# Attention scores from two fp32r parts in two 64-row tiles of the array, in a decoder layer on one core

## The chip, the cores and the metric

The kernel runs on one core of one Trainium2 chip. The metric is the device time of one execution in microseconds (us). A core has TensorE (PE in the profile; its weight loads are PEld), VectorE (DVE), ScalarE (ACT), GpSimd (POOL) and SyncE (SP), which here only issues transfers.

## The reference

A decoder layer with a layer norm behind each of three parts: causal self-attention, cross-attention to 64 context rows, and a mixture of 16 experts (4 picked per token) with one shared expert. The change touches the self-attention alone.

```python
# x: (2, 1024, 256); 16 heads of 16 columns
Q = einsum('bsd,hkd->bhsk', x, WQ)   # K, V alike
scores = einsum('bhqd,bhkd->bhqk', Q, K) / sqrt(16)
scores = where(causal, scores, -inf)
attn = einsum('bhqk,bhkv->bhqv', softmax(scores), V)
x = layernorm(x + einsum('bhsv,hdv->bsd', attn, WO))
x = layernorm(x + cross_attention(x, ctx, mask))
x = layernorm(x + experts(x))
```

## The kernel before

**Heads and groups.** The 2x16 heads are worked in `NG` = 8 groups of `HG` = 4. Q and K are projected in float32 (L1029), and their results are cut into three bfloat16 parts each: ACT copies PSUM to part 0 (L566), DVE subtracts it (L732, `rest`), ACT copies the rest to part 1 (L571), POOL subtracts again to part 2 (L443). SP stores each result to HBM (`qk_parts`, L373) and loads from there the stacks of a group (`load_stack`, L369): 16 rows per part, six pairs of parts under each other, `KR` = 96 rows. A matmul over the 96 rows gives Q times K from parts (`SPLIT_Q`, `SPLIT_K`), for one head.

**Two passes over the scores.** The softmax needs row maxima. The *A jobs* (PE L973) compute scores with queries on the partitions, add the causal mask on diagonal blocks with a matmul of the identity and a mask (L978), and DVE takes the negative maxima (L701). The maxima are cut in parts, transposed (*M*: L711 to L721 on DVE, L1001 on PE, L594 on ACT) and written by SP as three more rows under the Q stack (`KM` = 99). The *B jobs* (L991) compute the scores again with keys on the partitions, for a pair of heads into two banks; with the three extra rows they come out less their maximum; on diagonal blocks L994 adds the mask; ACT takes the exponential (L585). The *V products* (L1015) multiply with V in float32, four heads in four 32-column tiles of the array, each of them as two instructions in the profile.

**Order.** `step_order` writes out one group for all engines: 24 slots with one B job each, and in them the A jobs of the *next* group: a head of `A_HEAD` = 4, the other 34 spread over 18 slots. An A job is (query tile i, key half c, width w, first head, heads in a bank); there are 38 a group. They use three PSUM banks, `A_BANKS`, in turn; PE waits before job n for the maxima of jobs up to n-3 (L970). A V product follows every second slot from slot 3 on, M stands after slot 19. PE, ACT and DVE each run the same list in order. B job n waits for the exponential n-2. The A jobs of group 0 stand in the projection stage (`P1`), six in each half step of a Q or K projection.

**Loops.** `groups` runs group 0, then a hardware loop (`Fori`) with two passes of three groups, then group 7. `blocks` does the same for the experts: block 0 written out, a loop over blocks 1 to 3. SP loads the stacks two groups ahead.

Of the kernel before, what the change touches and what calls it, by code (L numbers as in the profile page):

```python
# [21 lines left out]
F32 = mybir.dt.float32  # L22
# [28 lines left out]
SPLIT_Q = (0, 1, 2, 0, 1, 0)  # L51
SPLIT_K = (0, 0, 0, 1, 1, 2)
KR = len(SPLIT_Q) * DH
KM = KR + 3
# [83 lines left out]
def build(nc, a, out, qk_parts, l_dram):  # L138
    with ExitStack() as ctx:
# [21 lines left out]
        qs = stacks[:, 8192:14336].bitcast(BF16).rearrange("p (u h s) -> p u h s", u=3, h=HG)  # L161
        ks = stacks[:, 14336:20480].bitcast(BF16).rearrange("p (u h s) -> p u h s", u=3, h=HG)
# [6 lines left out]
        parts = temps[:, 0:3072].bitcast(BF16).rearrange("p (u s t) -> p u s t", u=2, s=3)  # L169
        rest = temps[:, 3072:5120].rearrange("p (u t) -> p u t", u=2)  # L170
# [44 lines left out]
        nmx = sb("neg_max", [P, NC, HG, TB], F32)  # L215
        nm = sb("neg_m", [P, 2, HG * TB], F32)
        mparts = sb("m_parts", [P, 3, HG * TB], BF16)
        mrow = sb("m_rows", [3 * HG * TB, P], BF16)
# [21 lines left out]
        hs = nc.alloc_sbuf_tensor_at("h_split", [P, SPLIT_BUFS, 2, CH], F32R, offset=temps_at + 4 * 3072)  # L240
        ps = ctx.enter_context(nc.psum_tensor("ps", [P, 8, CH], F32))
# [11 lines left out]
        qk_ready, part_a, resid, part_b, part_c = (sem(n) for n in ("qk_ready", "part_a", "resid", "part_b", "part_c"))  # L253
# [45 lines left out]
        def groups(eng, run):  # L299

            run(0, 0, STEP0, 0)
            with eng.Fori(0, (NG - 2) // 3) as r:
                for s in range(3):
                    run(r * 3 + (s + 1), (s + 1) % 3, STEP, r + (s + 2) // 3)
            run(NG - 1, (NG - 1) % 3, LAST, 0)

        def blocks(eng, run):


            run(0, 2)  # L310
            with eng.Fori(1, T // CH) as c:
                run(c, 0)
# [34 lines left out]
        def _(sp):  # L347
# [13 lines left out]
            for dst, name in ((identb, "identb"), (causA, "causA"), (causB, "causB")):  # L361
                sp.dma_start(dst[:], a[name]).then_inc(ld_caus, 16)

            def load_stack(g):
                b, o, g2 = g // GB, g % GB // 2, g % 2
                for t, dst, split in ((0, qs, SPLIT_Q), (1, ks, SPLIT_K)):
                    for at, part in enumerate(split):
                        src = qk_parts[t, b, o, part, 64 * g2:64 * g2 + 64, :].rearrange("(h r) n -> r h n", h=HG)
                        sp.dma_start(dst[at * DH:(at + 1) * DH, g % 3], src).then_inc(ld_stack[g % 3], 16)  # L369

            for n, (b, o, t) in enumerate(QK):
                sp.wait_ge(part_c, n + 1)
                sp.dma_start(qk_parts[t, b, o].rearrange("s p n -> p s n"),  # L373
                             parts[:, n % 2]).then_inc(stored[n % 2], 16)
# [7 lines left out]
            for g in range(NG):  # L382
                sp.wait_ge(m_row, g + 1)
                for s in range(3):
                    n = HG * TB
                    sp.dma_start(qs[KR + s:KR + s + 1, g % 3].rearrange("o h s -> o (h s)"),
                                 mrow[s * n:(s + 1) * n, :]).then_inc(m_loaded, 16)
                if g == 0:
# [5 lines left out]
                    for dst, name in ((x, "x"), (wo1, "wo1"), (wxq, "wxq"), (wxk, "wxk"), (wxv, "wxv"),  # L394
                                      (wxo, "wxo"), (ctxT, "ctxT"), (bq, "bq"), (bk, "bk"), (bv, "bv"), (bo, "bo"),
                                      (gw, "gw"), (gb, "gb"), (mask_words, "mask"), (identf, "identf"), (hm, "hm")):
# [31 lines left out]
        def _(pool):  # L428

            nc.gpsimd.memset(ks[KR:P], 1.0).then_inc(filled, 1)  # L430
# [10 lines left out]
            for n in range(NQK):  # L441
                pool.wait_ge(part_b, n + 1)
                nc.gpsimd.tensor_tensor(parts[:, n % 2, 2, :], rest[:, n % 2, :], parts[:, n % 2, 1, :],  # L443
                                        ALU.subtract).then_inc(part_c, 1)
                g = n - 4
                if 0 <= g < 3:
                    pool.wait_ge(v_kept, NVJ // B)
# [847 lines left out]
```

## Time and profile before

| | us |
|---|---|
| median of 3 runs | 797.43 (796.6 to 802.91) |
| span of the profiled execution | 794.0 |
| projection stage, until the first B job | 0 to 79.5 |
| eight groups | 79.5 to 331 |
| the rest (output projection, cross-attention, experts) | 331 to 794 |

The span is that of one profiled execution, from its first to its last instruction. A time on a timeline row counts from the span's start. A matmul's record lasts longer than its columns take, since the pipeline is in it; how fast matmuls follow each other is read from their starts. Idle time in brackets is that of the engine ahead of the instruction, with what released it.

### The profile page before, as it was taken

What the parts mean: (1) busy time and instruction counts of PE and PEld (TensorE: products, weight loads), DVE (VectorE), ACT (ScalarE), POOL (GpSimd) and SP (SyncE); (2) the same over time, 40 slices, a digit from 0 to 9 for tenths busy, and PEclk for the clock granted to TensorE, in tenths of its full rate; (3) what the DMA queues carried; (4) which work ended last, traced back from release to release, by engine and by line L of the source; (5) the groups of instructions that cost most, each with busy time, mean ns of one, the idle gap of its engine ahead of it and who ended that gap; (6) DMA issues with size and microseconds to landing.
All of it is one profiled execution on the core that took longest, in us unless ns stands there. A gap on an engine that the chain in (4) does not pass through costs nothing.

```text
span 794.0 us, 13785 instructions
## 1 busy us (share of the span) xinstructions
PE 738.2 (93%) x4632; PEld 493.8 (62%) x4632; DVE 555.3 (70%) x1195; ACT 381.0 (48%) x639; POOL 280.6 (35%) x285
## 2 busy tenths in 40 slices
PE   6688999999699999988999998999999999999994
PEld 3345443443344443444777787877888888888883
DVE  1287867868386683195788774699778768777777
ACT  2222666566365667623544444654444544545441
POOL 8323001141204204223013223574445445545542
PEclk9989999999899999999999998999999999999998
DMA  4866951532506000080000000000000000000000
GB/s 150 161 164 158 254 104 27 84 63 37 96 4 96 17 3 18 17 320 32 1 2 1 1 1 1 1 2 1 1 1 14 13 0 0 26 0 0 7 20 27
DMA packets 21311, 38.23 MB, mean 48 GB/s; under 512 B 5768, under 2 KB 9320, under 8 KB 20872
## 3 DMA queue, kind: packets, MB, share of 16 engines
q1 hardware_dynamic: 19688, 35.32, 19.4%
q0 software_dynamic: 1568, 2.18, 1.2%
q8 instruction: 34, 0.56, 0.3%
q14 instruction: 21, 0.17, 0.1%
HBM read 28.64 MB, written 8.65 MB: 47 GB/s over the span
## 4 chain that ended last, share of the span: by engine, by line
PE 74%; DVE 13%; issue 5%; DMA 3%; ACT 3%; SPq 1%; POOL 1%; POOLq 0%; DVEq 0%; ACTq 0%
PE ps L1119 18%; PE ps L1217 9%; PE ps L1015 9%; PE ps L991 9%; PE ps L973 8%; PE ps L1137 4%; PE ps L1156 3%; DVE neg_max L701 3%; DVE x_tok L876 3%; PE ps L1146 2%; PE ps L1171 2%; PE ps L994 2%; PE ps L978 2%; PE ps L1029 2%; DMA stacks<-qk_parts 1%
## 5 line engine op out<-in xcount | busy, mean ns | idle before, releaser
L701 DVE TENSOR_REDUCE neg_max<-ps 128x1 f32<-128x512 f32 (+3 forms) x304 | 180.7, 655 | 72.0 <-PE ps L978 58.8
L1119 PE MATMUL ps<-x_split,w_split 128*128 (+1 forms) x816 | 201.6, 396 | 1.7 <-DVE temps L858 1.2
L585 ACT ACTIVATE temps<-ps 128x1024 f32<-128x1024 f32 (+1 forms) x192 | 149.0, 811 | 100.8 <-PE ps L994 74.3
L1119 PEld LDWEIGHTS ps<-x_split,w_split 128*128 128x128 f32 x816 | 149.9, 189 | 32.5 <-issue 2.5
L511 POOL TENSOR_TENSOR w_split<-stacks,w_split 128x512 fp32r<-128x512 f32 x70 | 90.8, 1297 | 130.3 <-ACT w_split L618 130.3
L973 PE MATMUL ps<-stacks 96*128 96x512 bf16 (+3 forms) x384 | 106.0, 334 | 21.6 <-issue 8.4
L1217 PE MATMUL ps<-w_split,h_split 128*128 128x256 f32 x816 | 110.5, 285 | 6.1 <-DVE x_tok L876 5.2
L1217 PEld LDWEIGHTS ps<-w_split,h_split 128*128 128x128 f32 x816 | 106.3, 190 | 15.0 <-issue 8.1
L876 DVE SCALAR_TENSOR_TENSOR x_tok<-ps,o_norm,x_tok 128x256 f32<-128x256 f32 x256 | 105.6, 475 | 0.1
L991 PE MATMUL ps<-stacks 99*128 99x512 bf16 (+3 forms) x384 | 99.9, 330 | 1.8 <-ACT temps L585 1.1
L624 ACT ACTIVATE temps<-ps 128x512 f32<-128x512 f32 x68 | 40.8, 599 | 112.9 <-PE ps L1119 112.7
L858 DVE TENSOR_TENSOR temps<-ps,temps 128x512 f32<-128x512 f32 x68 | 47.0, 691 | 60.9 <-ACT temps L624 60.6
L1015 PE MATMUL ps<-temps,v_group 128*32 128x512 f32 (+3 forms) x768 | 81.8, 498 | 0.0
L991 PEld LDWEIGHTS ps<-stacks 99*128 99x128 bf16 x384 | 33.8, 98 | 76.8 <-ACT temps L585 49.9
L973 PEld LDWEIGHTS ps<-stacks 96*128 96x128 bf16 x384 | 37.3, 100 | 61.9 <-DVE neg_max L701 25.5
L864 DVE TENSOR_TENSOR h_split<-temps,h_split 128x512 fp32r<-128x512 f32 x68 | 61.7, 908 | 6.3 <-ACT h_split L629 6.3
L505 POOL TENSOR_TENSOR ln_rstd<-ln_var_eps,minus_half 128x1 f32<-128x1 f32 x32 | 19.1, 598 | 122.8 <-DVE ln_var_eps L774 122.8
L518 POOL TENSOR_TENSOR w_split<-stacks,w_split 128x256 fp32r<-128x256 f32 x68 | 55.0, 809 | 13.8 <-ACT w_split L630 13.8
L629 ACT ACTIVATE h_split<-temps 128x512 fp32r<-128x512 f32 x68 | 43.1, 634 | 34.9 <-DVE temps L858 33.9
L978 PE MATMUL ps<-caus_a,ident_b 128*128 128x128 bf16 x256 | 51.1, 226 | 0.0
L994 PE MATMUL ps<-caus_b,ident_b 128*128 128x128 bf16 x256 | 50.2, 220 | 0.0
L643 ACT ACTIVATE temps<-temps 128x512 f32<-128x512 f32 x32 | 20.2, 631 | 50.8 <-DVE temps L890 50.8
(120 smaller groups left out, 887.3 us busy)
## 6 DMA issues: line engine op xcount, KB each, us to landing
stacks<-qk_parts SPq DMA_DIRECT2D x96, 128.0 KB, 5.7
qk_parts<-temps SPq DMA_DIRECT2D x8, 768.0 KB, 4.1
stacks<-in_w SPq DMA_DIRECT2D x1, 4352.0 KB, 14.0
stacks<-in_w SPq DMA_DIRECT2D x1, 2176.0 KB, 19.0
x_T<-in_xT SPq DMA_DIRECT2D x4, 512.0 KB, 8.9
x_tok<-in_x SPq DMA_DIRECT2D x1, 2048.0 KB, 12.4
out_tokens<-x_tok SPq DMA_DIRECT2D x16, 128.0 KB, 1.7
temps<-row_sums POOLq DMA_DIRECT2D x28, 64.0 KB, 2.6
```

The costliest lines, as they stand in the source:

```text
L511: nc.gpsimd.tensor_tensor(w13s[:, split_buf(n), 1].rearrange("p k n -> p (k n)"), w13[:, n % NE], w13s[:, split_buf(n), 0].rearrange("p k ...
L585: nc.scalar.activation(pt[:, n % 4, :, 0:w], ps[:, 2 + 2 * (n % 2):4 + 2 * (n % 2), 0:w], ACT.Exp, scale=SCALE).then_inc(b_exp, 1)
L701: nc.vector.tensor_reduce(nmx[:, c, h0:h0 + nh, i], ps[:, A_BANKS[n % 3], 0:w * nh].rearrange("p (h k) -> p h k", h=nh), axis=AX.X, op=ALU ...
L864: nc.vector.tensor_tensor(hs[:, split_buf(e), 1], hT[:, e % 2, :], hs[:, split_buf(e), 0], ALU.subtract).then_inc(h_lo, 1)
L876: nc.vector.scalar_tensor_tensor(x[:, t, :], y, comb[:, 1, t, e:e + 1], x[:, t, :], ALU.mult, ALU.add).then_inc(y_added, 1)
L973: last = nc.tensor.matmul(ps[:, A_BANKS[n % 3], w * s:w * s + w], qs[0:KR, ua, h0 + s, P * i:P * i + P], ks[0:KR, ua, h0 + s, CH * c:CH * ...
L978: last = nc.tensor.matmul(ps[:, A_BANKS[n % 3], w * (s + 1) - P:w * (s + 1)], identb[:], causA[:], start=False, stop=True)
L991: last = nc.tensor.matmul(ps[:, bank, 0:w], ks[0:KM, u, 2 * pr + s, P * j:P * j + P], qs[0:KM, u, 2 * pr + s, q0:q0 + w], start=True, stop ...
L994: last = nc.tensor.matmul(ps[:, bank, 0:P], identb[:], causB[:], start=False, stop=True)
L1015: last = nc.tensor.matmul(ps[HS * h:HS * h + HS, 6, CH - w:CH], vg[:, u, j, h, :], pt[:, (2 * p + h // 2) % 4, h % 2, 0:w], start=(j == 0) ...
L1119: last = nc.tensor.matmul(ps[:, 2 * part + e % 2, :], w13s[:, split_buf(e), wp, k, P * part:P * part + P], xs[:, bass.ds(c, 1), xp, k, :], ...
L1217: last = nc.tensor.matmul(ps[:, Y_BANKS[e % 2] + i // 2, D * (i % 2):D * (i % 2) + D], hs[:, split_buf(e), hp, P * i:P * i + P], w2s[:, sp ...
```

## The change

- Q and K are cut into two parts in fp32r (float32 storage, 4 bytes): ACT copies, DVE subtracts, and that is all. Three pairs of parts make `KR` = 48 rows, with two rows for the maxima `KM` = 50. A stack holds two heads side by side on the partitions: rows 0 to 63 and 64 to 127. The memory of a stack and the size of its load (twelve transfers of 128 KB) are the same; SP writes four rows of maxima, not three. A store of a projection grows from 768 KB to 1 MB.
- A score matmul reads 48 (50) rows of one half. The two heads of a pair follow each other as matmuls on rows 0 and 64, into two banks. Their mask matmuls (128 rows) come behind both; those of A take all blocks of a bank at once.
- An A job is now for a pair of heads and fills two banks, so there are 20 a group with 40 maxima; the head is 2 jobs, the rest one a slot, 3 in each half step of `P1`. PE waits before job n for maxima up to unit 2n-2.
- The chain of the maxima has three steps on DVE, not five; the transpose is float32.
- `Fori` is gone: seven groups and four expert blocks are written out. POOL's part of the cut is gone, its copies of V stand ahead in one piece, its first memset covers all of the K stack in float32.

```diff
-SPLIT_Q = (0, 1, 2, 0, 1, 0)
-SPLIT_K = (0, 0, 0, 1, 1, 2)
+SPLIT_Q = (0, 0, 1)
+SPLIT_K = (0, 1, 0)
 KR = len(SPLIT_Q) * DH
-KM = KR + 3
+KM = KR + 2
+ROWS = P // 2
+NPR = HG // 2
...
-            _n = min(HG, CH // _w)
-            A_JOBS += [(_i, _c, _w, _h, _n) for _h in range(0, HG, _n)]
+            _n = min(NPR, CH // _w)
+            A_JOBS += [(_i, _c, _w, _pr, _n) for _pr in range(0, NPR, _n)]
 NA = len(A_JOBS)
+NU = 2 * NA
-A_HEAD = 4
+A_HEAD = 2
...
-            with eng.Fori(0, (NG - 2) // 3) as r:
-                for s in range(3):
-                    run(r * 3 + (s + 1), (s + 1) % 3, STEP, r + (s + 2) // 3)
+            for g in range(1, NG - 1):
+                run(g, g % 3, STEP, (g + 1) // 3)
...
-            with eng.Fori(1, T // CH) as c:
+            for c in range(1, T // CH):
...
+                        src = qk_parts[t, b, o, part, 64 * g2:64 * g2 + 64, :].rearrange(
+                            "(pr d r) n -> d r pr n", pr=NPR, d=2)
+                        for d in range(2):
+                            rows = slice(ROWS * d + at * DH, ROWS * d + (at + 1) * DH)
+                            sp.dma_start(dst[rows, g % 3].bitcast(F32), src[d]).then_inc(ld_stack[g % 3], 16)
...
-            nc.gpsimd.memset(ks[KR:P], 1.0).then_inc(filled, 1)
+            nc.gpsimd.memset(ks[:].bitcast(F32), 1.0).then_inc(filled, 1)
...
-                nc.gpsimd.tensor_tensor(parts[:, n % 2, 2, :], rest[:, n % 2, :], parts[:, n % 2, 1, :],
-                                        ALU.subtract).then_inc(part_c, 1)
...
-                nc.scalar.activation(parts[:, n % 2, 1, :], rest[:, n % 2, :], ACT.Copy).then_inc(part_b, 1)
...
+                        for d in range(2):
+                            src = ps[:, A_BANKS[(2 * n + d) % 3], 0:w * npr].rearrange("p (h k) -> p h k", h=npr)
+                            nc.vector.tensor_reduce(nmx[:, c, d, pr:pr + npr, i], src,
+                                                    axis=AX.X, op=ALU.max, negate=True).then_inc(a_max, 1)
...
-                    dve.wait_ge(part_a, n + 1)
-                    if n >= 2:
-                        dve.wait_ge(part_c, n - 1)
+                    dve.wait_ge(part_hi, n + 1)
...
-                        wait(pe, a_max, (g + 1) * NA + (n - 1 if n < 2 else n - 2))
+                        wait(pe, a_max, (g + 1) * NU + max(2 * n - 1, 0))
                         diag = P * (i + 1) <= CH * (c + 1)
...
+                        banks = [A_BANKS[(2 * n + d) % 3] for d in range(2)]
+                        for s in range(npr):
+                            for d in range(2):
+                                rows = slice(ROWS * d, ROWS * d + KR)
+                                last = nc.tensor.matmul(ps[:, banks[d], w * s:w * s + w],
+                                                        qs[rows, ua, pr + s, P * i:P * i + P],
+                                                        ks[rows, ua, pr + s, CH * c:CH * c + w],
+                                                        start=(s == 0), stop=(s == npr - 1 and not diag))
+                        if diag:
+                            for d in range(2):
+                                edge = ps[:, banks[d], 0:w * npr].rearrange("p (h k) -> p h k", h=npr)[:, :, w - P:w]
+                                last = nc.tensor.matmul(edge, identb[:],
+                                                        causA[:].unsqueeze(1).to_broadcast([P, npr, P]),
                                                         start=False, stop=True)
...
+                        for d in range(2):
+                            rows = slice(ROWS * d, ROWS * d + KM)
+                            last = nc.tensor.matmul(ps[:, 2 + 2 * (n % 2) + d, 0:w], ks[rows, u, pr, P * j:P * j + P],
+                                                    qs[rows, u, pr, q0:q0 + w], start=True, stop=not diag)
+                        if diag:
+                            for d in range(2):
+                                last = nc.tensor.matmul(ps[:, 2 + 2 * (n % 2) + d, 0:P], identb[:], causB[:],
+                                                        start=False, stop=True)
```

## Rows read from the trace of the kernel before

**Rows 1.** The page's first part: busy us, share of the span, instructions.
```profile
PE 738.2 (93%) x4632; PEld 493.8 (62%) x4632; DVE 555.3 (70%) x1195; ACT 381.0 (48%) x639; POOL 280.6 (35%) x285
```

**Rows 2.** Windows: stretch, its length, busy us of each engine, clock, DMA.
```profile
112.00:140.00 28.00, 27.87 (x227) 11.80 (x229) 21.35 (x40) 18.62 (x26) 6.58 (x9) 1.00 0.37 58
300.00:330.00 30.00, 28.23 (x238) 10.31 (x236) 3.80 (x11) 23.80 (x34) 13.44 (x17) 1.00 0.08 22
```

**Rows 3.** L1001 on PE in three windows: durations, then first and last start.
```profile
L1001 PE MATMUL ps<-ident_b,m_parts x1: 257/257/257, 199.9 to 199.9; 128*96 128x128 bf16 x1
...
L1001 PE MATMUL ps<-ident_b,m_parts x1: 257/257/257, 240.3 to 240.3; 128*96 128x128 bf16 x1
...
L1001 PE MATMUL ps<-ident_b,m_parts x1: 257/257/257, 303.6 to 303.6; 128*96 128x128 bf16 x1
```

**Rows 4.** Timeline around the loop's jump: start, length, engine, what, idle before.
```profile
203.28 7.67 SPq L369 DMA_DIRECT2D stacks<-qk_parts  x12
207.31 0.23 PE L973 MATMUL ps<-stacks 96*128 96x128 bf16 x1 [3.50 <-issue]
...
211.76 0.27 PE L973 MATMUL ps<-stacks 96*128 96x128 bf16 x1 [4.05 <-issue]
```

**Rows 5.** Timeline of PE over one pair of slots.
```profile
128.52 1.06 PE L1015 MATMUL ps<-temps,v_group 128*32 128x512 f32 x8
129.52 0.60 PE L991 MATMUL ps<-stacks 99*128 99x512 bf16 x2
129.96 0.60 PE L973 MATMUL ps<-stacks 96*128 96x512 bf16 x2
...
131.35 0.22 PE L978 MATMUL ps<-caus_a,ident_b 128*128 128x128 bf16 x1
131.50 1.07 PE L1015 MATMUL ps<-temps,v_group 128*32 128x512 f32 x8
```

**Rows 6.** Timeline of PE in the head of a group.
```profile
140.48 0.23 PE L973 MATMUL ps<-stacks 96*128 96x128 bf16 x1
140.55 0.22 PE L978 MATMUL ps<-caus_a,ident_b 128*128 128x128 bf16 x1
...
142.00 0.34 PE L973 MATMUL ps<-stacks 96*128 96x384 bf16 x1 [0.20 <-DVE neg_max L701]
...
144.57 0.43 PE L1015 MATMUL ps<-temps,v_group 128*32 128x128 f32 x8
144.93 0.34 PE L991 MATMUL ps<-stacks 99*128 99x384 bf16 x1
```

**Rows 7.** Chain that ended last, in order of time: start, us, what.
```profile
471.10 1.69 PE ps L1189 x16
...
612.68 2.78 PE ps L1119 x12
615.47 1.43 PE ps L1217 x12
```

**Rows 8.** Timeline of DVE: the row maxima.
```profile
50.98 3.68 DVE L701 TENSOR_REDUCE neg_max<-ps 128x1 f32<-128x512 f32 x6 [0.63 <-PE ps L973]
...
130.38 1.29 DVE L701 TENSOR_REDUCE neg_max<-ps 128x1 f32<-128x512 f32 x2 [0.77 <-PE ps L973]
...
141.25 4.34 DVE L701 TENSOR_REDUCE neg_max<-ps 128x4 f32<-128x512 f32 x8 [4.71 <-PE ps L978]
```

**Rows 9.** Groups by form: busy us, mean ns, idle before and its releasers.
```profile
L701 DVE TENSOR_REDUCE neg_max<-ps 128x1 f32<-128x512 f32 x192 | 121.2, 682 | 17.5 <-PE ps L973 11.2 <-PE ps L978 6.0
...
L701 DVE TENSOR_REDUCE neg_max<-ps 128x1 f32<-128x384 f32 x64 | 32.0, 550 | 4.9 <-PE ps L978 4.8
```

**Rows 10.** Chain that ended last, in the projection stage.
```profile
20.25 1.07 ACT temps L571
21.38 2.14 POOL temps L443
23.54 3.55 DMA qk_parts<-temps
```

More of the change, by code:

```diff
@@ L360, in _ @@
             load_x(3)
[L361 removed]
+            for dst, name in ((identb, "identb"), (causA, "causA"), (causB, "causB"), (identf, "identf")):
                 sp.dma_start(dst[:], a[name]).then_inc(ld_caus, 16)
@@ L383, in _ @@
                 sp.wait_ge(m_row, g + 1)
[L384 to L387, printed above, removed]
+                for s in range(2):
+                    for d in range(2):
+                        n = NPR * TB
+                        at = ROWS * d + KR + s
+                        sp.dma_start(qs[at:at + 1, g % 3].rearrange("o pr s -> o (pr s)").bitcast(F32),
+                                     mrow[(2 * s + d) * n:(2 * s + d + 1) * n, :].bitcast(F32)).then_inc(m_loaded, 16)
                 if g == 0:
@@ L560, in _ @@
         def _(act):
-            def part_a_of(n):
+            for n in range(NQK):
                 act.wait_ge(qk_ready, n + 1)
@@ L592, in group @@
                         act.wait_ge(m_T, g + 2)
-                        wait(act, m_loaded, g * 48 + 48)
-                        nc.scalar.activation(mrow[:], ps[0:3 * HG * TB, 0, 0:64].bitcast(BF16),
-                                             ACT.Copy).then_inc(m_row, 1)
+                        wait(act, m_loaded, g * 64 + 64)
+                        nc.scalar.activation(mrow[:], ps[0:2 * HG * TB, 0, 0:P], ACT.Copy).then_inc(m_row, 1)
             groups(act, group)
@@ L985, in group @@
                         if n == 0:
-                            pe.wait_ge(m_loaded, g * 48 + 48)
+                            pe.wait_ge(m_loaded, g * 64 + 64)
                         wait(pe, b_exp, g * NB + n - 1)
                         diag = P * j >= CH * c
-                        for s in range(2):
-                            bank = 2 + 2 * (n % 2) + s
-                            last = nc.tensor.matmul(ps[:, bank, 0:w], ks[0:KM, u, 2 * pr + s, P * j:P * j + P],
-                                                    qs[0:KM, u, 2 * pr + s, q0:q0 + w], start=True, stop=not diag)
-                            if diag:
-                                last = nc.tensor.matmul(ps[:, bank, 0:P], identb[:], causB[:], start=False, stop=True)
+                        for d in range(2):
[3 more added lines that the diff above has]
+                        if diag:
+                            for d in range(2):
+                                last = nc.tensor.matmul(ps[:, 2 + 2 * (n % 2) + d, 0:P], identb[:], causB[:],
+                                                        start=False, stop=True)
                         last.then_inc(b_ready, 1)
```

104 lines of the change are left out of this document (39 added, 65 removed).

## Prediction

> **What bounds the kernel now.** I read the page's busy times first, then the windows, the times of one marker instruction, and last the timeline of TensorE (PE) and VectorE (DVE) in one attention group. Over the span PE is busy 93%, DVE 70%, ScalarE 48% [rows 1]. In the attention stage PE is busy 27.87 of 28.00 us, DVE 21.35 and ACT 18.62 [rows 2]. Only the last group differs: it has no A jobs, and there ACT has 23.80 us of 30 [rows 2].
>
> The transpose of the row maxima (L1001) runs eight times, once per group, and gives the period: 199.9 to 240.3 is 40.4 us, 240.3 to 303.6 is two groups of 31.65 us [rows 3]. The long one holds the jump back of the rolled loop: PE gets its next instructions 3.5 us late and stalls 4.05 us more inside the first A job, with nothing released by another engine, while twelve stack loads run [rows 4].
>
> The 31.65 us are PE's. In one pair of slots PE runs V (1.00 us), B, A, B, A without a hole: 131.50 minus 128.52 is 2.98 us [rows 5]. It is this pair that the change works on.
>
> **Prices from rows.** All in us.
> - A 512-column bf16 matmul streams in 0.217 (two in 0.43 to 0.44) [rows 5]; 128 columns with a mask matmul between take 0.06 each [rows 6].
> - fp32r runs at the same rate: 12 of 512 columns in 2.78. But 12 of 256 columns take 1.43, 0.119 each, and 16 of 16 columns with 128-column f32 weights 1.69, 0.106 each [rows 7]: below 256 columns a four-byte weight load sets the pace at 0.106.
> - V takes 0.36 at 128 columns and 1.00 at 512 [rows 5, 6]; the slope is (1.00-0.36)/384 = 1.67 ns a column, so 0.36 minus 0.213 = 0.15 is fixed. Before it, the last 128-column matmul started at 131.35 and was through at 131.41, V starts at 131.50: 0.09 more. V is the only place where the array changes its tiling (128x128 to 128x32 and back), so in costs 0.09 and out 0.15.
> - DVE: six 512-column maxima in 3.68 [rows 8], the first 0.68 long [rows 9], so 0.60 apart; 384 columns 0.55 long [rows 9]. 256 columns isn't in the trace; by those two I take 0.45.
> - Handing over: A matmuls at 129.96 and 0.22 later, DVE's first maximum at 130.38 [rows 5, 8]: 0.20 after the first one's last column. Back: DVE starts the first maximum at 141.25, ends it 0.68 later, and PE starts the A job that waited at 142.00 [rows 6, 8]: some 0.06.
>
> **The change part by part.**
> *Two heads at once.* Scores have 384+384 matmuls before and after; now neighbours lie in row tiles 0 and 64. I price a pair at 0.22 for any width: two weight loads of 0.106 one after the other, or 512 columns once. Bounds: 0.106 for narrow pairs if both tiles load at once, 0.43 if the tiles don't run together. The Trainium skill (TensorE: Matmul & The Clock Gate, Part 3) says that matmuls of different row groups start about 4 ns apart; no matmul of before uses a row tile, so no row here shows it, and the sum would be the same.
>
> *Switching.* Mask matmuls use all 128 rows. A diagonal job is now 64-row, 128-row, 64-row; 12 of 20 A jobs and 16 of 24 B jobs are diagonal. I take 0.09 in and 0.15 out, as at V [rows 5, 6], the nearest row; bounds are nothing, and 0.106 more at each pair where the weight load is exposed. The skill's page TensorEngine Tiling (Key Properties) says that changing the tiling mode drains the engine, which V's two gaps agree with; by it the switches cost, by a free change between row modes they don't, and that is a rival below.
>
> *Coarser A jobs.* This I take to be decisive. Before, 38 jobs use one bank each of three, and job n waits for the maximum n-3. Now a job fills two of the three banks, 20 jobs a group, and job n waits for unit 2n-2, the first half of the job just before it. PE can't be more than one job ahead. From one A job's last column to the next one's first column: 0.20+0.68+0.06 = 0.94. Then a pair: 1.16, raised to DVE's 2x0.60 = 1.20. A B job between hides in it (0.22, or 0.72 with its mask and three switches). In every second slot V stands between: 1.09+0.22+0.22 = 1.53. Two slots without masks: 2.73 to 2.98 before. The halved scores give 0.25 there, as PE's rest turns into waiting for DVE.
>
> With masks the steps grow. A job: 0.42 (pair 0.22, in 0.09, mask 0.11); a two-pair job 0.74; a B job after V 0.57 (0.42 and out 0.15). V with both gaps: 1.09, 0.88, 0.66, 0.45. The nineteen steps from A0 to A19: 1.45, 1.36, 1.23, 1.44, 1.36, 1.88 (V 1.09, B 0.57, A 0.22), 1.20, 2.19, 0.94, 1.20, 1.68, 1.20, 1.20, 1.73, 1.23, 1.53, 1.20, 2.08, 1.36: 27.5. The end without A: V 1.09+1.09+0.88+0.66, six B jobs 3x(0.57+0.42), the transpose 0.25 (now f32) and A0 0.74: 7.7. Together **35.2 a group, 3.5 more than 31.65; seven groups +24.5**. With free switches the same sum drops 0.09 at 11 diagonal A jobs, 0.24 at four B jobs after V, and 0.33 at each of three pairs in the end: 32.1. With the weight load exposed at some 35 places: +3.7, 38.9.
>
> *Last group.* In its slots of 512 columns without masks ACT binds [rows 2] and nothing changes. In its eight diagonal B couples the scores took 1.10, 0.88, 0.67, 0.46 by width and take 0.99 now: 2x(3.96-3.11) = **+1.7** (0 with free switches).
>
> *Loops written out.* No jump: 40.4 minus 31.65 = **-8.8**. Straight code of the first loop pass has stack loads beside it as well and no such stall; a second cost of this kind would show as another long period. The expert loops' cycle of 2.78+1.43 [rows 7] is PE's and stays. Without cover for the fetch it would cost as much again, +8.8.
>
> *Parts.* ACT's second copy (1.07) and POOL's subtraction (2.14) leave the chain ahead of the second store [rows 10]; the store grows from 0.75 to 1 MB, by a third of 3.55 = 1.2. So the first A job starts 2.1 earlier. The memset of k's stack has half the elements per partition and ends before the first split. The stack loads stay twelve of 128 KB a group; SP's row loads grow from 3 to 4, with the fourth behind the third for some 0.6, still ahead of the next group's first B. Then seven half steps of Q/K projection each with three coarse A jobs instead of six: PE returns with 1.7+0.22+0.20 after the last A, DVE had 0.2+1.28 of work, so it idles about 0.7 where it idled 0.63 [rows 8], and masked steps are 0.1 to 0.2 over DVE's own; some 0.3 each, +2.1. **Sum 0**, with -2.3 and +3 as bounds. The shorter maxima chain (three instead of five) gives 0.4 at places PE doesn't wait for.
>
> *Sum:* 794.0-8.8+24.5+1.7+0 = 811.4. The profiled span lies 3.4 below the median of the runs, 797.4; the forecast for the runs is **815**.
>
> **Rivals.**
> 1. *Row modes switch free.* 32.1 a group: 794.0-8.8+7x0.45-2.3 = 786.1, in the runs 789.5. With part of the price, up to 805. For it: only column tiles are seen to cost. Against: V pays in both directions.
> 2. *Faster: free switches and both tiles load weights at once.* Pairs of 128 and 256 columns take 0.106, of 384 0.16; on the path that gives about 1.2 a group, 30.9: 794.0-8.8-5.2-2.3 = 777.7, runs 781. It decides once a group takes less than 32: then the loop's 8.8 is kept. Against: weight loads of 0.106 are never seen side by side.
> 3. *The two tiles don't run together.* A pair costs 0.43; +0.65 in nine slot couples and 0.22x6 at the end, +7.2 on 35.2: seven groups +50, runs about 865.
> 4. *PE stays the only bound.* Then its sum would decide: scores 48x0.22, V 10.5, masks 3.5, about 25 a group, level with DVE's 40 maxima at 0.60; 794-8.8-7x6 = 743. It would need more than three banks for A.
>
> The clock stays at its upper level, 2.4 GHz, in my sum, as in the window of [rows 2].
>
> **How the numbers follow.** Forecast's case (switches cost about as V's, coarse A jobs) 0.55; rival 1 0.2; rival 2 0.14; rival 3 0.06; rival 4 0.05. The upper end: 38.9 a group, 794.0-8.8+50.8+2+3 = 841, runs 844; the lower end takes in rival 1 and most of what lies between it and rival 2: 783. This kernel's measurement tells about 1% from no change, 789.5 to 805.4. Slower: most of case one and rival 3, 0.58; within 1%: 0.21; faster: 0.21. Case one alone: 802 to 844.
>
> **What would show it.** L1001 seven times evenly spaced, no 40 us period (loop right). A period of 34 to 37 us; near 32 says that row switches are free; over 42 that tiles don't run together. In slots without V, PE idle before the A matmul with DVE's maximum as releaser, while DVE runs on at 0.60 a unit; in slots with V, DVE idle 0.3 to 0.5. A hole of 0.09 before and 0.15 after each mask pair. Two score matmuls of a pair starting within 0.11. If PE is still over 95% busy without holes, the step on the coarse jobs is wrong.

## The result, and the profile after

The changed kernel takes 908.4 us (median of 4 runs, 905.17 to 919.28), the kernel before 800.17 on the same chip: ratio 1.135, interval 1.128 to 1.142. The profiled execution of after is the longest of the four, 919.28 us, at a mean granted clock of 0.845 (the others have 0.861 to 0.871), so amounts taken from its trace are some 11 us high. The trace of before has a mean granted clock of 0.982.

The page of after: busy times, then TensorE's granted clock in 40 slices, then groups of instructions.

```profile
span 917.5 us, 12507 instructions
PE 852.2 (93%) x4568; PEld 520.3 (57%) x4568; DVE 563.9 (61%) x1195; ACT 377.0 (41%) x631; POOL 258.1 (28%) x277
...
PEclk9877558555965596559999999999999999999998
...
L695 DVE TENSOR_REDUCE neg_max<-ps 128x1 f32<-128x512 f32 (+3 forms) x320 | 188.9, 632 | 184.2 <-PE ps L969 139.0
L1009 PE MATMUL ps<-temps,v_group 128*32 128x512 f32 (+3 forms) x768 | 117.2, 694 | 0.1
```

The clock line of before, for comparison, is this:

```profile
PEclk9989999999899999999999998999999999999998
```

PE is 93% busy, as before [rows 1], and that share hides the change: it is now busy for 852 us instead of 738, with 64 instructions fewer. The digits of 5 in the clock line are slices at 1.2 GHz. Nine of the slices 5 to 18 have one, 92 to 413 us, and the groups lie there; from 85 to 424 us the mean granted clock is 0.64. The V product is the witness: it is the same instruction in both kernels, 768 times, and its mean is 694 ns where the page of before has 498. DVE idles 184 us ahead of the maxima (72 before), with PE as the releaser.

Windows of after: stretch, length, busy us of PE, PEld, DVE, ACT, POOL, granted clock, DMA. Below them the transpose of the maxima, once a group (L995, before L1001).

```profile
170.00:205.00 35.00, 33.98 (x157) 11.71 (x153) 14.30 (x26) 12.51 (x18) 6.99 (x9) 0.50 0.37 55
...
40.00:80.00 40.00, 30.82 (x83) 10.94 (x82) 24.85 (x39) 3.51 (x4) 0.00 (x0) 0.71 0.54 128
```
```profile
L995 PE MATMUL ps<-ident_f,m_parts x1: 273/273/273, 85.2 to 85.2; 128*64 128x128 f32 x1
...
L995 PE MATMUL ps<-ident_f,m_parts x1: 298/298/298, 424.5 to 424.5; 128*64 128x128 f32 x1
```

Seven periods take 424.5-85.2 = 339.3 us, against 7x31.65+8.8 = 230.4 before [rows 3]. They are uneven, 43.6 to 52.0. So the 123.5 us between the two spans are: ahead of the first transpose, which was at 73.1 before, +12.1; seven periods +108.9; all the rest +2.5.

Timeline of PE in after, first a stretch at the upper level, then one where the clock falls at about 161.5. Start, length, engine, what.

```profile
157.02 0.50 PE L983 MATMUL ps<-q_stack,k_stack 50*128 50x512 f32 x2
157.36 0.46 PE L962 MATMUL ps<-k_stack,q_stack 48*128 48x512 f32 x2
157.66 0.40 PE L983 MATMUL ps<-q_stack,k_stack 50*128 50x512 f32 x2
158.61 0.50 PE L962 MATMUL ps<-k_stack,q_stack 48*128 48x256 f32 x4 [0.55 <-DVE neg_max L695]
...
162.24 1.93 PE L1009 MATMUL ps<-temps,v_group 128*32 128x512 f32 x8
164.10 0.79 PE L983 MATMUL ps<-q_stack,k_stack 50*128 50x512 f32 x2
```

A pair of 512-column score matmuls (B L983, A L962) is followed by the next one after 0.34 and 0.30 us. One head after the other would take 0.43 [rows 5], so the two tiles do run together. PE then waits 0.55 for the maxima, as forecast for slots without V. But the V product takes 164.10-162.24 = 1.86 us, where it took 1.00 [rows 5].

### The profile page after: what moved, and what is told of

The parts are those of the page before. It is cut to its first block, busy times and chain, and to the rows that moved or that the text cites. A ratio compares the mean times of both kernels' runs of the same rounds, so it can differ in the third digit from the quotient of the medians.

```text
span 917.5 us, 12507 instructions
## 1 busy us (share of the span) xinstructions
PE 852.2 (93%) x4568; PEld 520.3 (57%) x4568; DVE 563.9 (61%) x1195; ACT 377.0 (41%) x631; POOL 258.1 (28%) x277
## 4 chain that ended last, share of the span: by engine, by line
PE 76%; DVE 14%; issue 4%; ACT 2%; DMA 2%; SPq 1%; POOL 0%; POOLq 0%; DVEq 0%; ACTq 0%
PE ps L1113 16%; PE ps L1009 11%; PE ps L962 10%; PE ps L1211 8%; PE ps L983 8%; DVE neg_max L695 5%; PE ps L969 4%; PE ps L987 3%; PE ps L1023 3%; PE ps L1131 3%; PE ps L1150 3%; DVE x_tok L862 2%; PE ps L1165 2%; PE ps L1140 1%; PE ps L1038 1%
## 5 line engine op out<-in xcount | busy, mean ns | idle before, releaser
L695 DVE TENSOR_REDUCE neg_max<-ps 128x1 f32<-128x512 f32 (+3 forms) x320 | 188.9, 632 | 184.2 <-PE ps L969 139.0
L1113 PE MATMUL ps<-x_split,w_split 128*128 128x512 f32 x816 | 200.9, 395 | 0.7 <-POOL w_split L510 0.5
L962 PE MATMUL ps<-k_stack,q_stack 48*128 48x512 f32 (+3 forms) x384 | 100.7, 551 | 31.3 <-DVE neg_max L695 25.2
L1009 PE MATMUL ps<-temps,v_group 128*32 128x512 f32 (+3 forms) x768 | 117.2, 694 | 0.1
L983 PE MATMUL ps<-q_stack,k_stack 50*128 50x512 f32 (+3 forms) x384 | 106.2, 551 | 1.9 <-ACT temps L578 1.4
L983 PEld LDWEIGHTS ps<-q_stack,k_stack 50*128 50x128 f32 x384 | 46.9, 242 | 106.3 <-issue 73.3
L962 PEld LDWEIGHTS ps<-k_stack,q_stack 48*128 48x128 f32 x384 | 45.7, 251 | 81.6 <-DVE neg_max L695 57.2
L621 ACT ACTIVATE h_split<-temps 128x512 fp32r<-128x512 f32 x68 | 43.1, 633 | 35.2 <-DVE temps L844 34.0
L1023 PE MATMUL ps<-x_T,w_qkv 128*128 128x512 f32 x64 | 40.1, 774 | 6.9 <-DMA x_T<-in_xT 6.9
L610 ACT ACTIVATE w_split<-stacks 128x512 fp32r<-128x512 f32 x70 | 43.6, 623 | 0.0
L987 PE MATMUL ps<-caus_b,ident_b 128*128 128x128 bf16 x256 | 43.0, 260 | 0.0
```

What stands on the lines that cost most here:

```text
L695: nc.vector.tensor_reduce(nmx[:, c, d, pr:pr + npr, i], src, axis=AX.X, op=ALU.max, negate=True).then_inc(a_max, 1)
L962: last = nc.tensor.matmul(ps[:, banks[d], w * s:w * s + w], qs[rows, ua, pr + s, P * i:P * i + P], ks[rows, ua, pr + s, CH * c:CH * c + w] ...
L983: last = nc.tensor.matmul(ps[:, 2 + 2 * (n % 2) + d, 0:w], ks[rows, u, pr, P * j:P * j + P], qs[rows, u, pr, q0:q0 + w], start=True, stop= ...
L987: last = nc.tensor.matmul(ps[:, 2 + 2 * (n % 2) + d, 0:P], identb[:], causB[:], start=False, stop=True)
L1009: last = nc.tensor.matmul(ps[HS * h:HS * h + HS, 6, CH - w:CH], vg[:, u, j, h, :], pt[:, (2 * p + h // 2) % 4, h % 2, 0:w], start=(j == 0) ...
L1023: last = nc.tensor.matmul(ps[:, 2 + 2 * (n % 2) + q, :], wqkv[:, k, D * t + P * o:D * t + P * o + P], xT[:, k, S * b + CH * q:S * b + CH * ...
```

## Experiments

The question is what lowers the clock, and what my sum is worth without it. Line numbers of a run are those of its own kernel; those of after and before shift by a few lines in them. Where an expected text speaks of theories by number: (1) what counts is how long columns stream, however many rows they use, and the halved streaming time lowers the clock; (2) it is the number of rows at work in the array; (3) it is the holes at each switch between row modes, the short pauses in which nothing streams. Theory 4 is told where it comes up. Unless a ratio is given, a kernel was run once; before took 794.6 to 803.0 us (medians) on the chips used.

### The loops alone

**b_unrolled**: before, with `groups` and `blocks` written out:
```diff
-            with eng.Fori(0, (NG - 2) // 3) as r: ...
+            for g in range(1, NG - 1):
+                run(g, g % 3, STEP, (g + 1) // 3)
-            with eng.Fori(1, T // CH) as c:
+            for c in range(1, T // CH):
```


> The kernel before with its two hardware loops written out, nothing else. My step on the loops: the period of 40.4 us that holds the jump becomes 31.65 as its neighbours, so 8.8 us less, some 791 in the runs, with the transposes of the maxima evenly spaced. Rival (the stall comes from the stack loads that start there, not from the jump): the long period stays, 800.

Measured: 791.62 us against 800.18, ratio 0.990 (0.983 to 0.997). The same transposes as [rows 3]:

```profile
L1000 PE MATMUL ps<-ident_b,m_parts x1: 257/257/257, 168.1 to 168.1; 128*96 128x128 bf16 x1
...
L1000 PE MATMUL ps<-ident_b,m_parts x1: 257/257/257, 199.6 to 199.6; 128*96 128x128 bf16 x1
...
L1000 PE MATMUL ps<-ident_b,m_parts x1: 257/257/257, 231.1 to 231.1; 128*96 128x128 bf16 x1
```

The period over the former jump is 31.5, like its neighbours, where it was 40.4: the step on the loops was right. That the medians give -8.6 for my -8.8 is partly luck. The two profiled executions, both at a mean clock of 0.982, lie 4.8 apart: 9.2 is gained up to the last transpose (303.6 to 294.4), and behind it the rest takes 494.8 where before takes 490.4. So the gain is some 5 to 9 us. This is the fastest of all the kernels here that compute the whole layer.

### Fewer streams, fewer rows: what the clock follows

**a_onetile**: after, with both heads of a pair read from rows 0 to 63 (the second head's scores are then those of the first), so that its matmuls run one after the other.
```diff
-                                rows = slice(ROWS * d, ROWS * d + KR)
+                                rows = slice(0, KR)
-                            rows = slice(ROWS * d, ROWS * d + KM)
+                            rows = slice(0, KM)
```


> The changed kernel with both heads of a pair read from rows 0 to 63, so that the two matmuls of a pair no longer run side by side (the second head's scores are then those of the first). 384 pairs stream twice as long. Theory 1: the clock comes back to 1.0 in most of the attention groups, and the time is not above the changed kernel's 908 although each pair takes 0.22 more at full clock, 860 to 900. Theory 2 (few rows in the array lower the clock): the clock stays at its lower level and the time rises by 384 times 0.43, to above 1000.

Measured: 1106.19 us, mean clock 0.728, period about 70.3. One window of it:

```profile
120.00:200.00 80.00, 79.45 (x288) 36.30 (x287) 27.75 (x50) 22.58 (x30) 2.34 (x3) 0.50 0.19 39
```

The two matmuls of a pair now follow each other, PE is busy for 79.45 of 80 us, and the clock is at 0.50 in all of this window. Streaming time alone, theory 1, doesn't explain it.

**a_btwice**: after, each pair of B matmuls issued twice (`for again in range(2)` around the pair).

> The changed kernel with the score matmuls of each B pair issued twice into the same banks (the second overwrites the first; the result is the same). Work added, nothing taken away: 192 pairs of 0.34 at full clock, 0.6 at half. Theory 1: the added streaming lifts the clock for part of the groups, and the time falls below 908, to 860 to 900. Theory 2 (tiles of 64 rows lower the clock) and theory 3 (the drains at the tile switches lower it): the clock stays low and the time rises by up to 115, to 980 or more.

Measured: 880.9 us, 27.5 less than after, with 384 matmuls more. Its clock line, and a window at either level:

```profile
PEclk9868659999999996599999999889999999999998
```
```profile
145.00:175.00 30.00, 28.67 (x226) 12.88 (x226) 22.78 (x39) 16.70 (x20) 3.40 (x6) 1.00 0.34 43
325.00:355.00 30.00, 29.45 (x193) 12.84 (x191) 12.39 (x23) 11.59 (x17) 5.48 (x7) 0.72 0.06 12
```

Five periods are 38.4, at the upper level, and two about 51, where it is lost. Added work made the kernel faster, because the clock was held for longer. This is what theory 1 foretold (860 to 900); theories 2 and 3, as I had put them, asked for 980 or more. So the rows aren't everything: how much is streamed over them counts too.

**b_48rows, b_64rows, b_66rows**: before, its score matmuls reading only the first 48, 64 or 66 of 96 (99) rows, which leaves out terms of the product and the subtraction of the maxima. With 64 rows or fewer a mask matmul starts 0.16 behind a score matmul of 128 columns, with 66 rows 0.05 to 0.06, as with 96: I read this as a 64-row tile against the whole array.
```diff
-                                                    qs[0:KR, ua, h0 + s, P * i:P * i + P],
-                                                    ks[0:KR, ua, h0 + s, CH * c:CH * c + w],
+                                                    qs[0:66, ua, h0 + s, P * i:P * i + P],
+                                                    ks[0:66, ua, h0 + s, CH * c:CH * c + w],
```


> The kernel before with its score matmuls reading 66 of the 96 (99) rows, so their sums leave out part of the terms; same columns, same order, same tiling (above 64 rows). Theory 1 (the clock goes with how long columns stream in a stretch; in the changed kernel two heads stream at once and PE waits for the maxima): clock and time as before, 800 and a mean granted clock of 0.98. Theory 2 (the clock goes with how many rows of the array take part): the granted clock falls in the attention groups and the time rises towards 880.

> The kernel before with its score matmuls reading 48 rows each (a 64-row tile; sums leave out part of the terms), one head after the other, masks in between as before. Price of the row tile alone. If a switch between 64 and 128 rows costs 0.24 for both ways, the 512 diagonal matmuls add 512x0.24 = 123: 920 at full clock, and more if the clock falls. If row modes switch free and rows don't matter: 800. If few rows lower the clock (theory 2) and switches are free: above 900 with a granted clock near 0.8.

> The kernel before with its score matmuls reading 64 rows, so that they use a 64-row tile where 66 rows (run b_66rows, 806) still use the whole array; one head after the other, sums leave out part of the terms. The only difference to b_66rows is the tiling: each diagonal head now goes from 64 rows to 128 and back. Price 0.24 for both ways, 512 times: 806+123 = 929 at full clock. If switches between row modes are free: 806. If the holes of the switches lower the clock, above 950.

Measured: 806.33 us with 66 rows (clock 0.969), 1090.89 with 64 (0.737), 1093.52 with 48 (0.737). PE of b_64rows at its start, PE of b_66rows in the same place, and a window of b_64rows later on:

```profile
86.98 0.23 PE L973 MATMUL ps<-stacks 64*128 64x128 bf16 x1
87.14 0.23 PE L978 MATMUL ps<-caus_a,ident_b 128*128 128x128 bf16 x1
```
```profile
79.31 0.22 PE L973 MATMUL ps<-stacks 66*128 66x128 bf16 x1
79.37 0.22 PE L978 MATMUL ps<-caus_a,ident_b 128*128 128x128 bf16 x1
```
```profile
120.00:200.00 80.00, 80.00 (x292) 21.36 (x290) 30.09 (x51) 24.95 (x31) 2.35 (x3) 0.50 0.14 21
```

Two things follow. A switch between a 64-row tile and the whole array costs 0.16-0.06 = 0.10 us, since without it the same pair of instructions lies 0.06 apart (b_66rows, and [rows 6] with 96 rows); the clock is at 1.00 in both stretches. And a PE that is busy for 80.00 of 80 us can be held at 1.2 GHz for all of them. With 66 rows the clock held (six periods of 31.6 to 31.8, as before), against theory 2, which asked for a time towards 880. From 66 to 64 rows the time jumps by 285 us. That could be the tile or the switches, so the masks had to go as well.

**b_allnomask, b_66nomask, b_64nomask**: before without its mask matmuls (the causal mask is left out), with all, 66 or 64 rows.
```diff
-                        diag = P * (i + 1) <= CH * (c + 1)
+                        diag = False
-                        diag = P * j >= CH * c
+                        diag = False
```


> The kernel before without the mask matmuls of the scores (no causal mask), all 96 and 99 rows kept. Against b_66nomask (887, clock 0.835) only the number of rows differs: no tile, no switch, the same matmuls in the same order. Theory 2 (rows at work in the array): full clock in the groups and 770 to 785. If the missing masks alone had lowered the clock in b_66nomask (theory 1, streaming time only): about 885 again.

> The same with 66 rows, in the whole array: what the masks' absence alone does to the clock and the time. Theories 3 and 4 both expect full clock but for the seam of the loop, and 806 less the masks' 64x0.057 a group, about 775 to 785, held up a little by the maxima on DVE.

> The kernel before with 64 rows a score matmul and no mask matmuls of the scores (no causal mask, and part of the terms left out). b_64rows lost the clock where b_66rows kept it; between them stand only the 64-row tile and its 1024 switches at the masks. Theory 3 (the holes at the switches are what lowered the clock there): without masks the clock is back at 0.95 or more and the time 775 to 800. Theory 4 (a matmul in a 64-row tile counts as half an array, with or without holes): the clock stays near 0.75 and the time above 950.

Measured: 770.94 us (clock 0.987), 887.32 (0.835) and 923.41 (0.800). The window 100 to 140 us, of b_allnomask and then of b_66nomask:

```profile
100.00:140.00 40.00, 37.17 (x260) 12.90 (x259) 29.16 (x58) 25.65 (x37) 7.19 (x9) 1.00 0.42 68
```
```profile
100.00:140.00 40.00, 39.95 (x156) 11.17 (x154) 19.02 (x36) 16.04 (x21) 2.35 (x3) 0.50 0.32 46
```

These two kernels differ in nothing but the rows that a score matmul reads, and neither has a switch between row modes in its scores. The one with 66 rows is 116 us slower (887.3 where before took 803.0 on that chip, 770.9 where it took 794.6), and its PE is the busier one. This is theory 2 by itself, in bf16, so it isn't a matter of fp32r either. It isn't a law, though: five of the seven periods of b_66nomask are 46 to 52 us and two are 31.3 and 31.5, nearly all at the upper level (0.94 and 0.93). With the masks, which use all 128 rows, 66 rows kept the clock at 0.969: the full-row mask matmuls helped to hold it, although they are extra work (806 against 887 us).

Theory 4, in the expected texts, is that a matmul in a 64-row tile counts as half an array. It asked for over 950 us without masks and for full clock with 66 rows, and both missed (923.4 and 0.835). Where both b_64nomask and b_66nomask have lost the clock, their periods are the same (46.4 and 50.5 each for the first two); the two periods in which 66 rows kept it make 38 us, about all of the 36 between the two times. With masks, b_64rows has periods of 69.8 at 0.50, 20 us above the 49.5 of b_64nomask, which is also at its lower level nearly throughout (0.53): 64 masks at 0.32, their own columns at half clock and two switches. So the mean clocks of these two, 0.737 and 0.800, tell how long the stretch at the lower level lasts, and not that one of them was held lower than the other. What makes 64 rows with masks lose the clock where 66 rows with masks hold it, the tile or the holes at its switches, these runs don't separate.

**a_nomask**: after without masks, so without those holes.

> The changed kernel without the mask matmuls of the scores (no causal mask on diagonal blocks; the sums are not the reference's). It takes away 28 mask pairs a group and 56 switches of tiling. Theory 3 (the holes of the switches lower the clock): the clock comes back to 0.98 and the time falls to 780 to 800. Theories 1 and 2 (too little of the array is at work): the masks used all 128 rows, so the clock stays low; the time falls only by the masks' own time, some 8 groups of 28x0.33 at half clock, to 835 to 860.

Measured: 868.61 us, clock 0.840. Periods fall to 37 to 44, but the clock doesn't rise. Theory 3 alone doesn't explain after. The run takes away the holes and the full-row mask matmuls together, and the second helped to hold the clock in b_66rows, so it doesn't say that the holes are harmless.

### The rows filled up

**a_64rows**: after, its score matmuls reading the whole 64-row tile (62 rows in the A jobs). The two rows of maxima stand at 62 and 63, the rows between are zero in the Q stack and one in the K stack, and the product is the same. The Q stack gets a memset. Matmuls, columns, switches and waits stay.
```diff
+MR = ROWS - 2
-                        at = ROWS * d + KR + s
+                        at = ROWS * d + MR + s
-                                rows = slice(ROWS * d, ROWS * d + KR)
+                                rows = slice(ROWS * d, ROWS * d + MR)
-                            rows = slice(ROWS * d, ROWS * d + KM)
+                            rows = slice(ROWS * d, ROWS * d + ROWS)
```


> The changed kernel with each score matmul reading its whole 64-row tile (62 rows for A): the two rows of the maxima move to rows 62 and 63, the rows between are zero in Q. Same columns, tiles, order and result; only more rows of the array take part. Theory 2 (few rows in the array lower the clock): the granted clock rises above 0.87 and the time falls, to 850 to 895. Theory 1 (only the time in which columns stream counts): 905 to 912 and the same clock.

Measured: 836.84 us against 799.92, ratio 1.045 (1.037 to 1.053); clock 0.972. The clock line, two windows, and two transposes:

```profile
PEclk9877799999999999999999999999999999999998
```
```profile
155.00:190.00 35.00, 31.64 (x246) 13.01 (x239) 23.43 (x44) 19.14 (x27) 7.00 (x9) 1.00 0.37 56
0.00:85.00 85.00, 63.22 (x176) 29.00 (x176) 35.13 (x56) 9.47 (x9) 17.79 (x15) 0.84 0.63 160
```
```profile
L999 PE MATMUL ps<-ident_f,m_parts x1: 298/298/298, 199.5 to 199.5; 128*64 128x128 f32 x1
...
L999 PE MATMUL ps<-ident_f,m_parts x1: 298/298/298, 235.6 to 235.6; 128*64 128x128 f32 x1
```

Rows of zeros, multiplied by ones, bring back the clock in the groups and 72 us of time. The period is now 36.1 or 36.2 in six cases of seven. The lower clock was worth 908.4-836.8 = 71.6 us of after, and here my sum can be held against a chip that runs as it assumed. The digits of 7 in slices 3 to 5 (42 to 104 us) are the projection stage and the start of the first group, which takes 39.6.

Two heads at once have 96 or 100 rows at work, no fewer than one matmul of before. But they don't follow each other every 0.217 as those do: a pair of 512 columns takes 0.23 to 0.34 (below), and PE waits for the maxima in between. The filled tile has the same pairs and waits. That few rows and pauses lower the clock together, so that either more rows (a_64rows) or more streaming (a_btwice) brings it back, is my reading of these runs; no single run shows it.

### What is in the 36 us

**a_fine** (from after) and **a_64fine** (from a_64rows): a bank of an A job is handed to DVE as soon as it is done (on a diagonal block behind its own mask matmul), and each bank is refilled as soon as DVE has read it, as before the change. For this the loops over heads and pairs change places, so that in a job of two pairs the heads no longer alternate.
```diff
-                        wait(pe, a_max, (g + 1) * NU + max(2 * n - 1, 0))
...
+                        for d in range(2):
+                            wait(pe, a_max, (g + 1) * NU + max(2 * n + d - 2, 0))
+                            for s in range(npr):
...
+                            if not diag:
+                                last.then_inc(a_ready, 1)
```


> The changed kernel with the A jobs handed over bank by bank: the first head's matmul waits for the maximum three banks back, not for the first half of the job before, and DVE starts on it while the second head's runs. My step on the coarse jobs: at full clock the steps without V lose nothing but the ones with V start up to 0.2 earlier, 2 to 3 a group. The clock may come back in some groups since PE waits less; 870 to 905. If the handing over doesn't matter (PE bound at half clock), 900 to 910.

> The changed kernel with full 64-row tiles and the A jobs handed over bank by bank. At full clock the last groups of a_fine ran at 35.3 a group where a_64rows takes 36.2: 7x0.9 = 6 less than a_64rows' 837, so 830; a little more where the clock of the projection stage comes back. If the coarse job were what holds the group, near 32 a group and 807.

**a_64nomask**: a_64rows without masks.

> The changed kernel with full 64-row tiles and without the mask matmuls of the scores (no causal mask on diagonal blocks; the sums are not the reference's). By my prices at full clock the period falls from the 36.2 of a_64rows to 29.9 (masks 0.11 and two switches of 0.24 together, 28 times, less what hides behind the maxima): time about 790. If row modes switched free, only the masks' 0.11 would go, 3 a group: 33 and 815.

Measured: a_fine 895.39 us (clock 0.866; groups at the upper level take 35.3), a_64fine 827.68 (0.972, period 35.3), a_64nomask 817.32 (0.922, period 30.8 at the upper level). For a_64nomask I had 790, and 815 if row modes switched free. The 815 is hit by luck: the period, 30.8, is that of the first case (29.9), but three of the seven are 37.3 to 38.7, at clocks of 0.69 to 0.72, which costs 22 us. So full tiles without the full-row masks don't hold the clock in every group. The window 199 to 235 us of a_64rows, of a_64fine and of a_64nomask, all at full clock:

```profile
199.00:235.00 36.00, 32.64 (x249) 13.36 (x249) 24.16 (x44) 20.04 (x27) 9.36 (x10) 1.00 0.36 53
```
```profile
199.00:235.00 36.00, 35.36 (x253) 15.69 (x253) 24.31 (x45) 20.05 (x27) 7.02 (x9) 1.00 0.39 58
```
```profile
199.00:235.00 36.00, 28.47 (x227) 11.38 (x227) 29.16 (x53) 23.16 (x33) 7.56 (x10) 1.00 0.41 61
```

By these windows PE is busy for 32.8 us of the 36.2 in a_64rows, for 34.7 of 35.3 in a_64fine and for 24.4 of 30.8 in a_64nomask. One group of before and one of b_allnomask, between two transposes, give the same without row tiles:

```profile
168.20:199.90 31.70, 31.34 (x259) 13.77 (x258) 23.73 (x44) 19.75 (x28) 9.36 (x10) 1.00 0.41 62
```
```profile
133.40:163.10 29.70, 28.05 (x193) 9.67 (x193) 23.64 (x44) 19.45 (x29) 7.00 (x9) 1.00 0.38 65
```

So the row tiles with two parts save 28.05-24.4 = 3.6 us of PE a group, and the masks, with their switches, cost 32.8-24.4 = 8.4 (0.30 for each of 28 diagonal jobs) where they cost 3.3 before. Together PE has 1.5 us more to do. The other 3 us of the longer period are PE's waits, 3.4 us a group where before has 0.4; 3.0 of them are for the maxima. This is the coarse handover, as forecast.

The fine handover gives back only 0.9, but it isn't a clean test of the coarse one, since it takes overlap away. A job of two pairs of 256 columns, up to its masks, in a_64rows and in a_64fine:

```profile
205.33 0.50 PE L966 MATMUL ps<-k_stack,q_stack 62*128 62x256 f32 x4 [0.52 <-DVE neg_max L699]
205.76 0.39 PE L973 MATMUL ps<-caus_a,ident_b 128*128 128x256 bf16 x2
```
```profile
198.49 1.05 PE L966 MATMUL ps<-k_stack,q_stack 62*128 62x256 f32 x4
199.47 0.39 PE L975 MATMUL ps<-caus_a,ident_b 128*128 128x256 bf16 x2
```

It takes 0.43 with the heads side by side and 0.98 without. That is part of why PE's busy time is 1.9 higher there.

A diagonal A job of a_64rows, and three pairs of a_64nomask behind a V product:

```profile
209.78 0.51 PE L966 MATMUL ps<-k_stack,q_stack 62*128 62x512 f32 x2
210.22 0.28 PE L973 MATMUL ps<-caus_a,ident_b 128*128 128x128 bf16 x2
210.44 0.44 PE L987 MATMUL ps<-q_stack,k_stack 64*128 64x384 f32 x2
```
```profile
239.14 0.50 PE L987 MATMUL ps<-q_stack,k_stack 64*128 64x512 f32 x2
239.47 0.40 PE L966 MATMUL ps<-k_stack,q_stack 62*128 62x512 f32 x2
239.71 0.40 PE L987 MATMUL ps<-q_stack,k_stack 64*128 64x512 f32 x2
```

The diagonal job takes 0.66, of which the two mask matmuls with the way back are 0.22; I had 0.42 and 0.15 for the way out, 0.57. The first pair behind V takes 0.33 and its record is 0.50 long; the next takes 0.24, with a record of 0.40. The two matmuls of a pair start 0.003 or 0.004 apart (278 of 288 pairs in six periods of a_64rows), so they run side by side, and 512 columns have the 0.22 of my price. The 0.10 more comes at a pair behind V, a mask or a wait, and fits one weight load that nothing hides; most of the 512-column pairs of a_64rows, 119 of 144 in six periods, are of this kind.

Not tried: the masks as 64-row matmuls too (two for each bank, one in either row tile), which would save the switches; the coarse handover refined without taking the pairs apart; and the changed kernel with its loops rolled up again.

## Why the prediction was wrong

The forecast was 815 us and slower; slower is right, 908.4 is far outside the range. Point by point:

- **The step that failed** is "The clock stays at its upper level, 2.4 GHz, in my sum". It was carried over from the window of [rows 2], where 96-row matmuls were at work. With 48 and 50 rows the granted clock is 0.64 in the mean of the groups, and 0.50 for long stretches. Filling the tiles gave back 71.6 of the 93.4 us that I missed by. In a_64rows only the rows that a matmul reads differ (and a memset at the start), so it is the rows; b_66nomask against b_allnomask, 887.3 to 770.9, shows the same without row tiles. None of the four rivals had the clock in it.
- The Trainium skill (TensorE: Matmul & The Clock Gate, Part 1) says that the clock is set by how busy TensorE has been. By it a PE that is 93% to 100% busy would stay at 2.4 GHz. The windows of b_64rows (80.00 of 80 us busy, 0.50) and b_66nomask (39.95 of 40, 0.50) show otherwise, if busy is read as time with an instruction in the engine; the measurement decides.
- *Loops written out*: right in the groups, 9.2 for 8.8; -8.6 in the medians, with the luck told above.
- *The period without the clock*: 36.2 for 35.2, where I had +3.5 over before and it is +4.5. The step on the coarse jobs holds as to its sign and about its size: PE is busy for 91% and waits 3.4 us a group, most of it for the maxima, with the foretold holes of 0.55. What I had too low is PE's own work. Rival 4 gave it as about 25 us, with no switch in it; it is 32.8. Scores and V were 48x0.22+10.5 = 21.1 for 24.4 measured (the exposed loads are part of this), masks and switches 3.5+28x0.24 = 10.2 for 8.4. On the path, taking the masks away is worth 36.2-30.8 = 5.4, where the expected text has 6.3.
- *Switches*: 0.10 between row modes (b_64rows), for my 0.09 and 0.15; the way back of 0.22 with its masks has one weight load in it. Rival 1 and rival 2 had them free. The bound "0.106 more at each pair where the weight load is exposed" came true at most wide pairs, and not only behind switches; that the period isn't the 38.9 of this bound fits its hiding in part behind PE's waits, which was not tested.
- *Two heads at once*: right. The two start 0.003 or 0.004 apart, and the pair takes 0.24, or 0.33 with a weight load exposed. Rival 3's 865 is nearest to the result and is still wrong: it asked for 0.43. A time near a rival's isn't evidence for its mechanism.
- *Projection stage*: I had a sum of 0. The first A job starts at 37.4 instead of 41.1, 3.7 earlier (I said 2.1; the store takes 4.01). Then it goes wrong. The chain of after, start, us and what:

```profile
20.20 4.01 DMA qk_parts<-qk_split
...
37.38 0.44 PE ps L962 x4
...
55.52 3.24 PE ps L1023 x4
58.76 0.58 PE ps L962 x2
59.36 1.29 DVE neg_max L695 x2
60.65 0.70 DVE neg_max L695
61.40 0.50 PE ps L962 x4
62.22 3.11 PE ps L1023 x4
```

Four projection matmuls take 2.7 to 3.5, where the chain of before has 1.72 to 1.77, since the clock is at 0.71 here. A half step takes 62.22-55.52 = 6.70. Before, these projections start 4.2 to 4.7 apart (44.60 to 66.47, five steps), so each half step is some 2.3 longer, and I had 0.3. Some 1.5 of it is the clock; the rest goes with PE's waits in the coarse A jobs, two of some 0.8 in a half step. The first transpose comes 12.1 late. In a_64rows this stretch is at 0.71 too, and the transpose 14.4 late (87.5). So filling the rows doesn't help here; PE waits for the maxima in between (30.82 of 40 us busy, where before has 34.09 and a clock of 0.94). Whether the waits or the fewer A matmuls lower the clock here was not taken apart.
- *The sum again, by a_64rows*: profiled span 833.8 against my 811.4, +22.4: projection stage +14.4, seven periods 256.7 for 246.2 (one of 39.6 right behind the projection stage, six of 36.2), the rest -2.5.

What stays open: how the rows and the streaming add up, and whether the holes at switches lower the clock by themselves. Few rows alone are shown to lower it (b_66nomask), full rows to bring it back (a_64rows), and full-row masks to help (b_66rows against b_66nomask; a_64rows against a_64nomask). Whether the holes hurt isn't shown: b_64rows against b_66rows changes the tile and the holes together. Also, a kernel holds the clock in one group and loses it in the next, with the same instructions (a_btwice, 38.4 and 51 us; b_66nomask, 31.3 and 47.0); what tips it was not found.

## What to carry to other kernels

Price a change to TensorE's work by rows too, not by columns alone: after it, look at the granted clock before anything else, and at an instruction that was not changed (here V, 498 to 694 ns). If a matmul must be short in rows, fill its tile with rows of zeros; a pair takes no longer for them, and they were worth 72 us here. Row tiles pay only where little with full rows stands between them: they saved 3.6 us of TensorE a group, and 28 mask pairs with their switches took 8.4 where the masks took 3.3 before. When a job gets coarser, count both: what its waits cost, and what TensorE itself has to do with every switch and every exposed weight load in it. And this hardware loop, whose jump back met a burst of loads, was worth writing out: 5 to 9 us, in a kernel that needed nothing else; before with its loops written out, 791.6 us, is the version to keep.

## What the hardware showed that I had not expected

- The granted clock fell to 1.2 GHz in a PE that was busy for 80.00 of 80 us (b_64rows), and for 39.95 of 40 with 66-row matmuls and no tiles at all (b_66nomask); 96 and 99 rows gave 1.00 in the same window (b_allnomask).
- Rows that hold zeros on one side count as rows at work (a_64rows, clock 0.972 for the 0.845 to 0.871 of after).
- A kernel got 27.5 us faster by issuing 384 matmuls twice (a_btwice).
- Two matmuls in two 64-row tiles start 0.003 or 0.004 apart, and the pair of 512 columns takes 0.24, where one matmul alone takes 0.217 [rows 5] and two in turn 0.43. Behind V, a mask or a wait the pair takes 0.33.
